# An expert's outputs in the other order: the 64-row half made and added first, the 128-row half second

## The chip, the cores and the metric

The kernel runs on one core of one Trainium2 chip. The metric is the time of one launch on the device in microseconds (us); of several runs the median counts, and less is better. A core has five engines that follow their own instruction streams and meet at semaphores only: PE (TensorE, matrix products; its weight loads are listed as PEld), DVE (VectorE), ACT (ScalarE), POOL (GpSimd) and SP (SyncE). Sixteen DMA engines move data between the chip's memory (DRAM) and the on-chip memory; SP issues the plain loads (queue q1 of the profile), POOL the indirect ones (queue q0).

## The reference

One decoder layer over 32 sequences of 128 tokens, width 512: a normed differential attention with rotary embedding, a cross attention to a context of 128 rows per sequence, and a mixture of experts. Cut to the part that the change touches, the mixture of experts does this for its T = 4096 tokens and E = 48 kept experts:

```
logits = x @ gate_weight.T                    # experts that are not kept: -inf
top_v, top_i = top_k(softmax(logits), 8); top_v /= sum(top_v)
xb[e, 0:192] = the first 192 tokens that chose expert e      # capacity 192
g, u = split(xb @ gate_up_proj.T);  h = silu(g) * u          # 192 wide
y = h @ down_proj.T                                          # 512 wide
out[token] += weight * y                                     # over the chosen experts
```

All numbers are FP32. A token can be among several experts' rows, so two experts' additions can meet in one row of the output.

## The kernel before

It has two stages. The first (up to about 690 us) takes the 32 sequences through attention, cross attention and routing, one sequence per turn, several sequences in flight. It writes the residual rows to the output in DRAM and scatters each token's record (normed row, weights, token number) to the slots of its experts. The second stage takes the 48 experts, and the change lies there alone.

An expert has 192 slots, cut into a half of 128 rows (h = 0) and a half of 64 rows (h = 1). Each engine runs `expert_turn` once per turn; in one turn the engines work on three experts at once: `t` (rows are transposed and split), `u` (gate and up product, L1382, and the activation) and `d` (down product, L1416). FP32 products are made from a high and a low part, which is why every operand is copied (ACT, L693) and its rest subtracted (DVE, L1133).

The way of an expert's outputs:

- PE (L1405 to L1418) makes both halves one after the other, five products each, in two banks of its result memory: half 0 in bank 4 (128 rows), half 1 in bank 5 (64 rows). It counts each half on the semaphore `down_tensor`; the object `dwn_t` (L355) names the order of the counts. Before it overwrites a bank it waits until that half of the expert before was copied out.
- ACT (L821 to L825) copies half 0 to the buffer `y` (called qk_both in the profile) and scales it with the slots' weights; DVE (L1172 to L1177) does the same for half 1. `y` has room for two experts, so both wait until the additions of the expert before the last are through (`d_add`, L824 and L1175).
- POOL (L680 to L687) adds the rows to the output in DRAM with one indirect DMA for each half (`add_outputs`, L670 to L678): each row goes to the row of its token, and the DMA adds. Since two experts can meet in a row, POOL waits at L683 until both additions of the expert before have landed. The order is: that wait, the wait for half 0, its addition, the wait for half 1, its addition.

SP loads each expert's data ahead: `load_gate_up` (L436, 768 KB), `load_down` (L442, 256 KB), `load_rows` (L454 and L456, 280.5 and 140.2 KB). Each waits until its buffer is free, which DVE signals (L1141, L1181, L1193). The order on every engine is as written in the code; nothing is moved by a scheduler.

Of the kernel before, what the change touches and what calls it, by code (L numbers as in the profile page):

```python
# [86 lines left out]
def decoder_layer(nc, x, ctx_rows, ctx_t, mask, weights, lambdas, subln, gate, gate_up, down_proj,  # L87
# [9 lines left out]
    with stack:  # L97
# [254 lines left out]
        ffn_a = Steps(sem("rows_scalar"), "high0 high1")  # L352
        ffn_v = Steps(sem("rows_vector"), "low0 low1")
        ffn_w = Steps(sem("rows_vector_kept"), "tokens weight")
        dwn_t = Steps(sem("down_tensor"), "y0 y1")  # L355
        dwn_v = Steps(sem("down_vector"), "y1")
        dwn_a = Steps(sem("down_scalar"), "y0")

# [195 lines left out]
        def _(pool):  # L554
# [125 lines left out]
            for e in range(E):  # L680
                d = Batch(e // 2, e % 2, E)
                if d.back(1).exists():
                    pool.wait_ge(d_add[d.back(1).parity], moved(d.back(1), 2))  # L683
                pool.wait_ge(dwn_a.sem, dwn_a.after(d, "y0"))
                add_outputs(d, 0)
                pool.wait_ge(dwn_v.sem, dwn_v.after(d, "y1"))
                add_outputs(d, 1)  # L687

        @block.scalar
        def _(act):  # L690
# [101 lines left out]
            def expert_turn(b):  # L792
                t, u, d = b["turn"], b["up"], b["down"]
                if t.exists():
                    act.wait_ge(d_gu[t.parity], moved(t, 1))
                    if t.back(2).exists():
                        act.wait_ge(gup_t.sem, gup_t.after(t.back(2), "second"))
                    copy(gu_high[:, t.parity, :, :], gu_sb[:, t.parity, :, :], wgu_a)
                if u.exists():
                    act.wait_ge(gup_t.sem, gup_t.after(u, "first"))  # L800
                    if u.back(1).exists():
                        act.wait_ge(gup_v.sem, gup_v.after(u.back(1), "h2"))
                    act.activation(silu1[:, :], ps[:, 2, 0:CAP], ACT.Silu).then_inc(gup_a.sem, 1)
                    act.wait_ge(gup_t.sem, gup_t.after(u, "second"))
                    act.activation(silu2[:, :], ps[0:INTER - P, 3, 0:CAP], ACT.Silu).then_inc(gup_a.sem, 1)
                if t.exists():
                    for h in range(2):
                        act.wait_ge(ffn_t.sem, ffn_t.after(t, f"rowsT{h}"))
                        if t.back(2).exists():
                            act.wait_ge(gup_t.sem, gup_t.after(t.back(2), "second"))  # L810
                        copy(rows_high[:, t.parity, :, part(h)],
                             ps[:, h, 0:KC * PART[h]].rearrange("p (c n) -> p c n", c=KC), ffn_a)
                if u.exists():
                    if u.back(2).exists():
                        act.wait_ge(dwn_t.sem, dwn_t.after(u.back(2), "y1"))
                    for h, dst, name in ((h1, h1_high, "h1"), (h2, h2_high, "h2")):
                        act.wait_ge(gup_v.sem, gup_v.after(u, name))
                        copy(dst[:, u.parity, 0, :], h[:, :], gup_a)
                    copy(h2_again[:, u.parity, 0, :], h2[:, :], gup_a)
                if d.exists():  # L820
                    act.wait_ge(dwn_t.sem, dwn_t.after(d, "y0"))  # L821
                    act.wait_ge(ffn_w.sem, ffn_w.after(d, "weight"))
                    if d.back(2).exists():
                        act.wait_ge(d_add[d.back(2).parity], moved(d.back(2), 2))  # L824
                    copy(y[:, d.parity, 0, :], ps[:, 4, :], dwn_a, scale=weight_of[d.parity][:, 0:1])  # L825
                if u.exists():
                    act.wait_ge(d_dn[u.parity], moved(u, 1))
                    if u.first():
                        act.wait_ge(d_dn2, 16 * 3)
                    if u.back(2).exists():  # L830
                        act.wait_ge(dwn_t.sem, dwn_t.after(u.back(2), "y1"))
                    copy(dn_high[:, u.parity, 0, :], dn_sb[:, u.parity, :], wdn_a)
                    copy(dn2_high(u), dn2_raw(u), wdn_a)
            expert_turns(act, expert_turn)
# [2 lines left out]
        def _(dve):  # L837
# [297 lines left out]
            def expert_turn(b):  # L1135
# [24 lines left out]
                                rows_high[:, t.parity, :, part(h)]).then_inc(ffn_v.sem, 1)  # L1160
                if u.exists():
                    if u.back(2).exists():
                        dve.wait_ge(dwn_t.sem, dwn_t.after(u.back(2), "y1"))
                    dve.wait_ge(gup_a.sem, gup_a.after(u, "high1"))
                    left_by(h1_low[:, u.parity, 0, :], h1[:, :], h1_high[:, u.parity, 0, :]).then_inc(gup_v.sem, 1)
                    dve.wait_ge(gup_a.sem, gup_a.after(u, "high2"))
                    if u.first():
                        for parity in range(2):
                            dve.memset(h2_rest[HALVES[1 - parity], parity, 0, :].bitcast(FP32), 0.0)
                    left_by(h2_low(u), h2[:, :], h2_high[:, u.parity, 0, :]).then_inc(gup_v.sem, 1)  # L1170
# [28 lines left out]
        def _(pe):  # L1199
# [165 lines left out]
            def expert_turn(b):  # L1365
                t, u, d = b["turn"], b["up"], b["down"]
                if u.exists():
                    if u.first():
                        keep_busy(2, 6)
                    if u.is_(1):  # L1370
                        keep_busy(3, 6)
                    pe.wait_ge(wgu_v.sem, wgu_v.after(u, "low"))
                    pe.wait_ge(ffn_v.sem, ffn_v.after(u, "low1"))
                    if u.back(1).exists():
                        pe.wait_ge(gup_v.sem, gup_v.after(u.back(1), "h2"))

                    def gate_up_block(dst, m):
                        cols = slice(m * P, (m + 1) * P)
                        pairs = [(gu_high, rows_high), (gu_high, rows_low), (gu_low, rows_high)]
                        for n, (left, right) in enumerate(pairs):  # L1380
                            for k in range(KC):
                                last = pe.matmul(dst, left[:, u.parity, k, cols], right[:, u.parity, k, :],  # L1382
                                                 start=(n == 0 and k == 0), stop=(n == 2 and k == KC - 1))
                        return last
                    for m in range(2):
                        last = gate_up_block(ps[:, 2, m * CAP:(m + 1) * CAP], m)
                    last.then_inc(gup_t.sem, 1)
                    gate_up_block(ps[:, 3, 0:CAP], 2).then_inc(gup_t.sem, 1)
                if t.exists():
                    if t.first():  # L1390
                        keep_busy(18)
                    pe.wait_ge(d_rows[t.parity], moved(t, 2))
                    if t.back(1).exists():
                        pe.wait_ge(ffn_v.sem, ffn_v.after(t.back(1), "low1"))
                    for h in range(2):
                        for c in range(KC):
                            n = PART[h]
                            last = pe.transpose(ps[:, h, c * n:(c + 1) * n], rows[0:n, t.parity, h, c * P:(c + 1) * P],
                                                ident[0:n, 0:n])
                        last.then_inc(ffn_t.sem, 1)  # L1400
                if d.exists():
                    pe.wait_ge(wdn_v.sem, wdn_v.after(d, "low2"))
                    pe.wait_ge(gup_v.sem, gup_v.after(d, "low2"))
                    pe.wait_ge(gup_a.sem, gup_a.after(d, "again"))
                    for h in range(2):  # L1405
                        if h == 0:
                            if d.back(1).exists():
                                pe.wait_ge(dwn_a.sem, dwn_a.after(d.back(1), "y0"))
                        else:
                            if d.back(1).exists():  # L1410
                                pe.wait_ge(dwn_v.sem, dwn_v.after(d.back(1), "y1"))
                        dst = ps[0:PART[h], 4 + h, :]
                        pairs = [(h1_high, dn_high, P), (h1_high, dn_low, P), (h1_low, dn_high, P),
                                 (h2_twice, dn2_both, P), (h2_rest, dn2_both, P)]
                        for i, (left, right, n) in enumerate(pairs):
                            last = pe.matmul(dst, left[0:n, d.parity, 0, part(h)], right[0:n, d.parity, 0, :],  # L1416
                                             start=(i == 0), stop=(i == len(pairs) - 1))
                        last.then_inc(dwn_t.sem, 1)  # L1418
# [55 lines left out]
```

## Time and profile before

| | us |
|---|---|
| median of 3 runs | 1086.99 (1086.17 to 1087.95) |
| the profiled execution | 1082.65 |
| its span, first to last instruction | 1080.9 |
| first addition of outputs starts | 704.27 |
| last addition of outputs starts | 1075.11 |

Over the whole span PE is busy for 94%, DVE for 77%, ACT for 58%, POOL for 54%. These shares are means over two stages with different limits, so they do not tell what limits the expert stage. The page also follows the work that ended last backwards to what released it; there 52% of the span is PE's and 22% is the additions to the output (layer_out), in flight as DMAs. An addition appears in the profile twice: as POOL's instruction at L672, which lasts while POOL writes the DMA's orders, and as the DMA itself, whose time is told from the start of that instruction to its landing.

### The profile page before, as it was taken

What the parts mean: (1) busy time and instruction counts of PE and PEld (TensorE: products, weight loads), DVE (VectorE), ACT (ScalarE), POOL (GpSimd) and SP (SyncE); (2) the same over time, 40 slices, a digit from 0 to 9 for tenths busy, and PEclk for the clock granted to TensorE, in tenths of its full rate; (3) what the DMA queues carried; (4) which work ended last, traced back from release to release, by engine and by line L of the source; (5) the groups of instructions that cost most, each with busy time, mean ns of one, the idle gap of its engine ahead of it and who ended that gap; (6) DMA issues with size and microseconds to landing.
All of it is one profiled execution on the core that took longest, in us unless ns stands there. A gap on an engine that the chain in (4) does not pass through costs nothing.

```text
span 1080.9 us, 24325 instructions
## 1 busy us (share of the span) xinstructions
PE 1020.4 (94%) x6564; PEld 830.6 (77%) x6564; DVE 832.9 (77%) x2255; ACT 625.6 (58%) x1751; POOL 579.1 (54%) x565
## 2 busy tenths in 40 slices
PE   5999999999999999999999987999999999999993
PEld 3787778878878788778787875788888787877882
DVE  5678778878888788788887865588888878778782
ACT  4555455455455554554555541477767676676772
POOL 3224665676666666766666666434444343443444
PEclk9999999999999999999999999999999999999997
DMA  7999674543313112122134132489999999989984
GB/s 285 370 294 265 248 262 158 212 153 129 131 56 99 49 54 92 49 81 65 49 97 166 55 122 79 135 234 257 239 248 234 239 235 230 247 217 238 240 203 58
DMA packets 90644, 185.75 MB, mean 172 GB/s; under 512 B 23943, under 2 KB 24071, under 8 KB 89712
## 3 DMA queue, kind: packets, MB, share of 16 engines
q1 hardware_dynamic: 59232, 145.13, 41.2%
q0 software_dynamic: 31376, 40.20, 18.0%
q8 instruction: 16, 0.26, 0.1%
q14 instruction: 20, 0.16, 0.0%
HBM read 116.04 MB, written 122.00 MB: 220 GB/s over the span
## 4 chain that ended last, share of the span: by engine, by line
PE 52%; DMA 27%; issue 10%; POOL 5%; DVE 3%; ACT 1%; SPq 0%; POOLq 0%; DVEq 0%
PE ps L1226 27%; DMA layer_out<-qk_both,slot_table 22%; PE ps L1211 9%; PE ps L1216 4%; DMA arena<-in_x 4%; PE ps L1253 3%; PE ps L1324 2%; POOL layer_out L672 2%; PE ps L1357 2%; POOL slot_records L587 2%; PE ps L1382 2%; PE ps L1416 1%; DMA gu_sb<-in_weights 1%; POOL rstd L598 1%; DMA arena<-slot_records 1%
## 5 line engine op out<-in xcount | busy, mean ns | idle before, releaser
L587 POOL DMA_INDIRECT slot_records<-row,slot_idx x240 | 245.2, 1022 | 78.5 <-issue 50.0
L672 POOL DMA_INDIRECT layer_out<-qk_both,slot_table x96 | 161.6, 1683 | 223.2 <-DMA layer_out<-qk_both,slot_table 196.0
L598 POOL TENSOR_TENSOR rstd<-mv,neg_half 128x1 f32<-128x1 f32 x96 | 67.8, 707 | 121.4 <-DVE mv L966 78.5
L1226 PE MATMUL ps<-w_high,xn_high 128*128 128x512 f32 x384 | 114.1, 419 | 0.7 <-ACT xn_high L693 0.7
L728 ACT ACTIVATE arena<-ps,neg_max 128x128 f32<-128x128 f32 x256 | 90.1, 378 | 33.4 <-DVE neg_max L958 33.4
L1226 PE MATMUL ps<-w_low,xn_high 128*128 128x512 f32 x384 | 107.7, 403 | 0.0
L1226 PE MATMUL ps<-w_high,xn_low 128*128 128x512 f32 x384 | 106.7, 399 | 0.0
L1382 PE MATMUL ps<-w_high 128*128 128x192 f32 x576 | 89.7, 278 | 13.4 <-DVE w_low L1133 13.0
L1382 PEld LDWEIGHTS ps<-w_high 128*128 128x128 f32 x576 | 76.7, 191 | 30.2 <-issue 28.3
L1133 DVE TENSOR_TENSOR w_low<-gu_sb,w_high 128x1536 fp32r<-128x1536 f32 x48 | 84.4, 1758 | 16.1 <-ACT w_high L693 14.9
L693 ACT ACTIVATE xn_t<-ps 128x512 f32<-128x512 f32 x64 | 38.3, 599 | 98.9 <-PE ps L1211 98.8
L1382 PE MATMUL ps<-w_high,w_low 128*128 128x192 f32 x576 | 87.8, 274 | 0.0
L1382 PE MATMUL ps<-w_low,w_high 128*128 128x192 f32 x576 | 87.7, 274 | 0.0
L1416 PE MATMUL ps<-w_high 128*128 128x512 f32 x192 | 80.4, 419 | 2.6 <-DVE w_high L1133 2.6
L1226 PEld LDWEIGHTS ps<-w_low,xn_high 128*128 128x128 f32 x384 | 70.9, 191 | 14.1
L1226 PEld LDWEIGHTS ps<-w_high,xn_low 128*128 128x128 f32 x384 | 70.1, 189 | 13.6
L643 POOL TENSOR_TENSOR arena<-qk_both 128x256 f32<-128x256 f32 x64 | 46.5, 745 | 60.0 <-DVE qk_both L1048 60.0
L1211 PEld LDWEIGHTS ps<-ident,arena 128*128 128x128 f32 x392 | 43.3, 142 | 43.5 <-ACT arena L693 17.0
L1048 DVE TENSOR_TENSOR qk_both<-ps,rope_tab 128x1024 f32<-128x1024 f32 x64 | 75.2, 1217 | 1.2 <-PE ps L1226 1.2
L1382 PEld LDWEIGHTS ps<-w_low,w_high 128*128 128x128 f32 x576 | 75.9, 192 | 0.0
L1382 PEld LDWEIGHTS ps<-w_high,w_low 128*128 128x128 f32 x576 | 75.9, 192 | 0.0
L1211 PE MATMUL ps<-ident,arena 128*128 128x128 f32 x392 | 61.9, 284 | 14.1 <-ACT arena L740 8.9
(164 smaller groups left out, 2477.0 us busy)
## 6 DMA issues: line engine op xcount, KB each, us to landing
gu_sb<-in_gate_up SPq DMA_DIRECT2D x48, 768.0 KB, 5.9
slot_records<-arena SPq DMA_DIRECT2D x6, 3366.0 KB, 25.0
arena<-slot_records SPq DMA_DIRECT2D x48, 280.5 KB, 4.4
dn_sb<-in_down_proj SPq DMA_DIRECT2D x48, 256.0 KB, 3.7
arena<-in_x SPq DMA_DIRECT2D x32, 256.0 KB, 2.7
x_res<-in_x SPq DMA_DIRECT2D x32, 256.0 KB, 3.0
ctx_t_sb<-in_ctx_t SPq DMA_DIRECT2D x32, 256.0 KB
ctx_sb<-in_ctx_rows SPq DMA_DIRECT2D x32, 256.0 KB
```

The source lines that it names most:

```text
L587: pool.indirect_dma_start(out=records, out_offset=bass.IndirectOffsetOnAxis(ap=slot_idx_of(s)[:, k:k + 1], axis=0), in_=row_of(s), in_offs ...
L598: pool.tensor_tensor(rstd[:, :], mv[:, 1:2], neg_half[:, 0:1], ALU.pow).then_inc(steps.sem, 1)
L643: pool.tensor_tensor(qk_rot[:, g, 1, :], qk_cos[:, g, 1, :], qk_sin[:, g, 0, :], ALU.add).then_inc(rope_p.sem, 1)
L672: pool.indirect_dma_start(out=out, out_offset=bass.IndirectOffsetOnAxis(ap=slot_table[0:PART[h], 2 * d.index + h:2 * d.index + h + 1], axi ...
L728: last = act.activation(probs[:, s, h, :], blocks(banks_s[:, s, :])[:, h, :], ACT.Exp, bias=neg_max[:, s, h:h + 1], accum_out=prob_sum[:, ...
L1048: dve.tensor_tensor(buf[:, :, :, :].rearrange("p (a g) r f -> p a (g r) f", a=2), qk, rope_tab[:, i, :, :].unsqueeze(2).to_broadcast([P, 2 ...
L1133: return dve.tensor_tensor(dst, src, high.bitcast(FP32), ALU.subtract)
L1211: last = pe.transpose(blocks(bank)[:, c, :], src(c), ident[:, :])
L1216: last = pe.matmul(dst, left(c), right(c), start=(c == 0), stop=(c == n - 1))
L1226: last = pe.matmul(dst, left[:, c, :], right[:, m, c, :], start=(n == 0 and c == 0), stop=(n == 2 and c == KC - 1))
L1382: last = pe.matmul(dst, left[:, u.parity, k, cols], right[:, u.parity, k, :], start=(n == 0 and k == 0), stop=(n == 2 and k == KC - 1))
L1416: last = pe.matmul(dst, left[0:n, d.parity, 0, part(h)], right[0:n, d.parity, 0, :], start=(i == 0), stop=(i == len(pairs) - 1))
```

## The change

The two halves of an expert's outputs change places, in what PE makes first and in what POOL adds first. The counts of `down_tensor` are renamed to match, so that ACT still waits for half 0 and DVE for half 1, and so that "both halves are made" is still the second count (now called y0). ACT's and DVE's own order is as before.

```diff
-        dwn_t = Steps(sem("down_tensor"), "y0 y1")
+        dwn_t = Steps(sem("down_tensor"), "y1 y0")
...
                 if d.back(1).exists():
                     pool.wait_ge(d_add[d.back(1).parity], moved(d.back(1), 2))
+                pool.wait_ge(dwn_v.sem, dwn_v.after(d, "y1"))
+                add_outputs(d, 1)
                 pool.wait_ge(dwn_a.sem, dwn_a.after(d, "y0"))
                 add_outputs(d, 0)
-                pool.wait_ge(dwn_v.sem, dwn_v.after(d, "y1"))
-                add_outputs(d, 1)
...
                     if u.back(2).exists():
-                        act.wait_ge(dwn_t.sem, dwn_t.after(u.back(2), "y1"))
+                        act.wait_ge(dwn_t.sem, dwn_t.after(u.back(2), "y0"))
...
                     if u.back(2).exists():
-                        dve.wait_ge(dwn_t.sem, dwn_t.after(u.back(2), "y1"))
+                        dve.wait_ge(dwn_t.sem, dwn_t.after(u.back(2), "y0"))
...
-                    for h in range(2):
+                    for h in (1, 0):
                         if h == 0:
                             if d.back(1).exists():
                                 pe.wait_ge(dwn_a.sem, dwn_a.after(d.back(1), "y0"))
```

On POOL, at the start of the second stage, the additions of the first three experts stood in this order before. A row is one addition; down_scalar is the signal that half 0 (128 rows) was copied out, down_vector that of half 1 (64 rows), and outputs_added the landing of the expert before.

```order
L672 DMA layer_out<-qk_both,slot_table 4352x512 [waits residual_stored1,residual_stored0,down_scalar]
L672 DMA layer_out<-qk_both,slot_table 4352x512 [waits down_vector]
L672 DMA layer_out<-qk_both,slot_table 4352x512 [waits down_scalar,outputs_added0]
L672 DMA layer_out<-qk_both,slot_table 4352x512 [waits down_vector]
L672 DMA layer_out<-qk_both,slot_table 4352x512 [waits down_scalar,outputs_added1]
```

The same place in the changed kernel:

```order
L672 DMA layer_out<-qk_both,slot_table 4352x512 [waits residual_stored1,residual_stored0,down_vector]
L672 DMA layer_out<-qk_both,slot_table 4352x512 [waits down_scalar]
L672 DMA layer_out<-qk_both,slot_table 4352x512 [waits down_vector,outputs_added0]
L672 DMA layer_out<-qk_both,slot_table 4352x512 [waits down_scalar]
L672 DMA layer_out<-qk_both,slot_table 4352x512 [waits down_vector,outputs_added1]
```

The wait for the landing of the expert before now stands in front of the 64-row addition, and the 128-row addition is the last of each expert.

On PE, in an expert's turn, the down product stood before as follows, between the transposes of a later expert's rows (L1398) and the next turn's first gate product (L1382). The number of rows is the first of the two sizes.

```order
L1398 MATMUL ps<-ident,arena 128x64 x4
L1416 MATMUL ps<-w_high 128x512
L1416 MATMUL ps<-w_low,w_high 128x512
L1416 MATMUL ps<-w_high,w_low 128x512
L1416 MATMUL ps<-w_high 128x512
L1416 MATMUL ps<-w_high,w_low 128x512
L1416 MATMUL ps<-w_high 64x512
L1416 MATMUL ps<-w_low,w_high 64x512
L1416 MATMUL ps<-w_high,w_low 64x512
L1416 MATMUL ps<-w_high 64x512
L1416 MATMUL ps<-w_high,w_low 64x512
L1382 MATMUL ps<-w_high 128x192 x4
```

In the changed kernel:

```order
L1398 MATMUL ps<-ident,arena 128x64 x4
L1416 MATMUL ps<-w_high 64x512
L1416 MATMUL ps<-w_low,w_high 64x512
L1416 MATMUL ps<-w_high,w_low 64x512
L1416 MATMUL ps<-w_high 64x512
L1416 MATMUL ps<-w_high,w_low 64x512
L1416 MATMUL ps<-w_high 128x512
L1416 MATMUL ps<-w_low,w_high 128x512
L1416 MATMUL ps<-w_high,w_low 128x512
L1416 MATMUL ps<-w_high 128x512
L1416 MATMUL ps<-w_high,w_low 128x512
L1382 MATMUL ps<-w_high 128x192 x4
```

The five products of the 64-row half moved ahead of the five of the 128-row half; the instructions are the same.

## Rows read from the trace of the kernel before

**Rows 1.** Busy time by stretch of the expert stage (columns named in the first row)

```profile
core 0: us, PE busy (x) PEld busy (x) DVE busy (x) ACT busy (x) POOL busy (x), PEclk, DMA share, GB/s
704.00:742.00 38.00, 38.00 (x283) 33.31 (x282) 31.77 (x62) 29.44 (x58) 15.89 (x9) 1.00 0.90 236
742.00:1048.00 306.00, 292.82 (x2108) 247.09 (x2107) 246.19 (x468) 217.35 (x427) 130.38 (x78) 1.00 0.93 237
1048.00:1081.00 33.00, 15.53 (x102) 12.21 (x100) 12.32 (x25) 11.25 (x23) 15.33 (x10) 0.82 0.49 68
```

**Rows 2.** Instructions of L672 over the span, what POOL waited for (us, times)

```profile
L672 POOL DMA_INDIRECT layer_out<-qk_both,slot_table x96: 1424/1567/2188, 704.3 to 1075.1; - x96
...
  DMA layer_out<-qk_both,slot_table: 196.0, 47
```

**Rows 3.** Chain that ended last (start us, us, what it was)

```profile
738.52 2.51 PE ps L1416 x10
...
850.70 5.84 DMA layer_out<-qk_both,slot_table
...
1062.60 4.18 DMA layer_out<-qk_both,slot_table
```

**Rows 4.** Timeline of POOL (start us, us, instruction, idle time before and what ended it)

```profile
704.27 1.57 POOL L672 DMA_INDIRECT layer_out<-qk_both,slot_table  x1 [12.57 <-ACT qk_both L695]
...
848.83 1.56 POOL L672 DMA_INDIRECT layer_out<-qk_both,slot_table  x1 [4.24 <-DMA layer_out<-qk_both,slot_table]
850.70 1.72 POOL L672 DMA_INDIRECT layer_out<-qk_both,slot_table  x1 [0.30 <-issue]
856.80 1.57 POOL L672 DMA_INDIRECT layer_out<-qk_both,slot_table  x1 [4.38 <-DMA layer_out<-qk_both,slot_table]
...
1047.92 1.56 POOL L672 DMA_INDIRECT layer_out<-qk_both,slot_table  x1 [3.84 <-DMA layer_out<-qk_both,slot_table]
...
1060.74 1.56 POOL L672 DMA_INDIRECT layer_out<-qk_both,slot_table  x1 [3.07 <-DMA layer_out<-qk_both,slot_table]
1062.60 1.43 POOL L672 DMA_INDIRECT layer_out<-qk_both,slot_table  x1 [0.30 <-issue]
1067.04 1.56 POOL L672 DMA_INDIRECT layer_out<-qk_both,slot_table  x1 [3.02 <-DMA layer_out<-qk_both,slot_table]
```

**Rows 5.** Instructions of L672, 848.5 to 849.5 us: one 128-row addition's landing

```profile
DMA to landing us min/median/max: 4.8/4.8/4.8
```

**Rows 6.** Instructions of L672, 1060 to 1061 us: the same near the end

```profile
DMA to landing us min/median/max: 4.9/4.9/4.9
```

**Rows 7.** DMA queues, 851 to 852.5 us (packets, MB, share of 16 engines)

```profile
q0 software_dynamic: 87, 0.18, 95.6%
q1 hardware_dynamic: 1, 0.00, 0.0%
```

**Rows 8.** DMA queues, 854 to 855.25 us

```profile
q1 hardware_dynamic: 110, 0.23, 54.0%
q0 software_dynamic: 63, 0.11, 47.4%
```

**Rows 9.** Timeline, all engines: loads and copies around one expert, and the first expert

```profile
703.09 0.73 DVE L1133 TENSOR_TENSOR w_low<-h,w_high 128x192 fp32r<-128x192 f32 x2
703.30 0.69 ACT L695 ACTIVATE qk_both<-ps,weight_even 128x512 f32<-128x512 f32 x1
...
850.57 0.33 SPq L442 DMA_DIRECT2D dn_sb<-in_down_proj  x1
...
853.53 0.34 SPq L436 DMA_DIRECT2D gu_sb<-in_gate_up  x1
...
856.56 0.69 ACT L695 ACTIVATE qk_both<-ps,weight_even 128x512 f32<-128x512 f32 x1 [1.77 <-DMA layer_out<-qk_both,slot_table]
856.56 0.74 DVE L1176 TENSOR_SCALAR qk_both<-ps,weight_even 64x512 f32<-64x512 f32 x1 [0.86 <-DMA layer_out<-qk_both,slot_table]
```

**Rows 10.** The page's slices of the span, 27 us each: memory traffic

```profile
GB/s 285 370 294 265 248 262 158 212 153 129 131 56 99 49 54 92 49 81 65 49 97 166 55 122 79 135 234 257 239 248 234 239 235 230 247 217 238 240 203 58
```

More of the change, by code:

```diff
@@ L830, in expert_turn @@
                     if u.back(2).exists():
-                        act.wait_ge(dwn_t.sem, dwn_t.after(u.back(2), "y1"))
+                        act.wait_ge(dwn_t.sem, dwn_t.after(u.back(2), "y0"))
                     copy(dn_high[:, u.parity, 0, :], dn_sb[:, u.parity, :], wdn_a)
```

## The prediction

> **What bounds the kernel now.** I first read the chain of work that ended last. After PE's last down product there, at 738.52 us, it names nothing but additions to the output in flight, each followed by a short step on POOL; the reader sees one such addition per expert [rows 3]. The instructions of L672 say the same from POOL's side: of its 48 experts, 47 began after a wait for a landing of the expert before, 196.0 us in all [rows 2]. So the 48 pairs of additions form one chain from 704.27 us to the end. Third, the timeline of POOL gives one link of it: the first addition starts at 848.83 us, issues for 1.56 us, the second starts 0.31 us later at 850.70, lands 5.84 us after its start, at 856.54, and 0.26 us later POOL starts the next expert at 856.80 [rows 3, 4]. That is 0.26 + 1.56 + 0.31 + 5.84 = 7.97 us. Over the first 43 experts the mean is (1047.92 - 704.27) / 43 = 7.99 us; near the end, with no loads left, it is 1067.04 - 1060.74 = 6.30 us [rows 4].
>
> What matters in that sum is which landing ends it. The 128-row addition, issued first, lands 4.8 us after its start [rows 5], at 853.6; POOL does not wait for that, since the 64-row one lands 2.9 us later.
>
> The copies to `y` are ready in time: at 856.56 ACT and DVE copy out an expert after waiting 1.77 and 0.86 us for the very landing that also frees POOL [rows 9]. PE is close behind with 292.82 of 306 us busy between 742 and 1048 us, the DMA engines with a share of 0.93 [rows 1]. Neither gives the beat now, but both are near enough to be rivals.
>
> **The change part by part.** It removes no instruction and no byte. It decides which addition is issued last.
>
> *The first issue gets shorter, the second longer.* Without loads the 64-row issue takes 1.43 us and the 128-row one 1.56 us [rows 4]: -0.13 us at the first place, +0.13 us within the landing time of the second. In the loaded stretch the second issue took 1.72 us for 64 rows [rows 4], 0.29 more than near the end; I take this as bound to the place, so whichever half stands there pays it. If it grows with the rows, 0.29 us more per expert.
>
> *The last landing is now that of 128 rows.* Near the end I have both sizes nearly undisturbed: 4.9 us for 128 rows [rows 6], 4.18 for 64 [rows 3]. An expert's link there becomes -0.13 + (4.9 - 4.18) = +0.59 us longer. For the 43 loaded experts no row shows a 128-row addition in the second place, so I bound it. From below: the extra 64 rows cost no more than undisturbed, +0.59 us. From above: the loaded 64-row landing is 5.84 - 4.18 = 1.66 us longer than the undisturbed one, of which the issue is 0.29 and the crowd 1.37; if twice the rows meet twice the crowd, +0.59 + 1.37 = +1.96 us. A gain is excluded as long as rows take DMA time at all; the rival below says what if they don't.
>
> Between these ends the row on the queues decides. While the first addition's rows move, they have the engines nearly alone: q0 95.6%, the loads' q1 0.0% [rows 7]. While the second one's rows move, q0 has 47.4% and q1 54.0% [rows 8], since the load issued at 850.57 has begun and the 768 KB load issued at 853.53 is about to [rows 9]. So the small half moves into the free stretch, where nobody waits for it, and the large half into the shared one. At that share the extra rows need 0.59 / 0.47 = 1.26 us. The share does not hold for the whole of a longer transfer, as the loads pause between two issues, so I take the middle of 0.59 and 1.26, 0.93 us.
>
> The Trainium skill, "DMA: Bandwidth & Descriptors", "Queues, rings and completion order", says that a DMA engine takes turns between queues and drains a whole packet, typically 9 to 17 descriptors, before it switches. An expert's rows on one engine would then pass in one go, and the crowd would be met once: the lower end, +0.59 us, and 1116 us in all. The trace shows only that both queues hold about half over 1.25 us [rows 8], not in what grain.
>
> *PE's order.* PE makes the 64 rows first. ACT's copy of half 0 becomes possible later by the five products of the other half; in the loaded stretch ACT waits 1.77 us for the landing anyway [rows 9], which covers it, and the copy runs a whole expert ahead of POOL. Uncovered it would hold up ACT's weight copies behind it by about 1.25 us, half of the 2.51 us that the ten products of both halves take [rows 3]. The renamed waits still ask for the second count, so DVE's and ACT's splits of a later expert wait as before. SP's waits are untouched.
>
> *The first addition.* Before, it waited for ACT's copy at 703.30 [rows 4, 9]. Now it needs DVE's copy, and DVE is busy with two subtractions from 703.09 for 0.73 us [rows 9], then copies for 0.74: POOL starts at about 704.8 instead of 704.27, +0.5 us once.
>
> *Sum.* 0.5 + 43 x 0.93 + 5 x 0.59 = 0.5 + 40.0 + 3.0 = 43.5 us. Against the profiled execution's own 1082.65 us (1080.9 of span and 1.75 around it) that is 1126.1; the median of the runs is 4.3 us above that execution, so 1086.99 + 43.5 = 1130 us.
>
> **The rivals.**
> 1. *Only the bytes count.* The extra 128 KB move at the fastest rate that a slice shows, 370 GB/s [rows 10], in 0.35 us; per expert +0.35, in all 0.5 + 48 x 0.35 = 17 us, 1104 us. For: the slices of the expert stage lie below that rate. Against: the undisturbed landings differ by 0.72 us, of which only 0.13 is issue. The Trainium skill, same page, "Anatomy of one DMA — SWDGE (gpsimd) path", has a fit of this kind, 2.0 us plus the bytes over 436 GB/s; as an estimate it puts the extra rows at 0.30 us, and 0.5 + 48 x 0.30 = 15 us in all. The trace speaks against it by the same 0.72 us.
> 2. *Faster: the crowd sets the last landing, not the rows.* Of the 5.84 us, 1.66 are there only in company. If the second addition ends when the loads let its last row through, however many rows it has, then only the shorter first issue is left: 0.5 - 48 x 0.13 = -5.7 us, 1081 us. It decides from the point where 64 more rows lengthen the landing by under 0.13 us. For: the loads' queue holds over half there [rows 8]. Against: near the end, with no loads, the rows do cost 0.59 us.
> 3. *No change: the DMA engines set the beat.* A share of 0.93 of 7.99 us is 7.4 us of transfers per expert; were that the limit, their order would not matter, 1087 us. For: the share [rows 1]. Against: POOL waits 47 times for a landing, also near the end, where the share is 0.49 [rows 1, 2].
> 4. *Much slower.* Twice the rows meet twice the crowd, +1.96 us: 0.5 + 43 x 1.96 + 3 = 88 us, 1175 us. PE would then idle some 2 us per expert; its granted clock is 1.00 through the stage and 0.82 only over the last 33 us, of which it is busy for 15.5 [rows 1], so a fall of the clock to its lower level, 1.2 GHz, would belong to this case.
>
> **How the numbers follow.** The forecast, from +0.59 to about +1.6 us per expert (1116 to 1160 us), gets 0.74; rival 1 0.08, rival 2 0.07, rival 3 0.06, rival 4 0.05. What this measurement can tell from no change is about 0.2%, 2 us. Faster is rival 2, 0.07; same is rival 3, 0.06; slower is the rest, 0.87. The range from 1104 to 1160 us holds the forecast and most of rival 1, about 8 in 10.
>
> **What would show it.** In the changed profile the first issue should take 1.43 us; near the end a link of 6.9 us instead of 6.30, its last landing 4.9 us after the start of the 128-row addition; in the loaded stretch a link of about 8.9 us, with the last landing about 6.9 us after that start; the DMA share between 742 us and the end of the loads near 0.83 (7.43 us of transfers in 8.92), PE idle for more than a tenth of it at a granted clock of 1.00. The prediction is wrong if the loaded link stays at 8.0 us, if POOL waits for a copy instead of a landing, or if loads move in time so that the 128 rows find the engines free.

## The result, and the profile after

The changed kernel takes 1113.82 us (median of 6 runs, 1108.84 to 1115.08) against 1086.93 for the kernel before: a ratio of 1.0239, 95% interval 1.0218 to 1.0260, so 24 to 28 us slower. The forecast was 1130 us, range 1104 to 1160.

The profiled span grew by more than the medians, from 1080.9 to 1112.8 us. Of these 31.9 us, 3.41 lie before the first addition, which starts at 707.68 us and not at 704.27. Most of that is not the change's: PE's first down product already starts 2.81 us later there, and in profiles of kernels that make and add the 128-row half first, this first addition starts anywhere between 704 and 710 us.

The expert stage by stretch (columns as in [rows 1]):

```profile
707.00:745.00 38.00, 37.96 (x283) 32.97 (x282) 31.35 (x61) 28.63 (x56) 13.50 (x8) 1.00 0.90 234
745.00:1077.00 332.00, 294.25 (x2111) 246.82 (x2110) 248.78 (x469) 214.66 (x430) 120.10 (x78) 1.00 0.88 220
1077.00:1113.00 36.00, 16.38 (x99) 12.66 (x97) 12.71 (x25) 11.30 (x23) 15.54 (x10) 0.78 0.45 62
```

Nearly the same work takes 332 us in place of 306. PE is idle for 11% of it where it was idle for 4, at a granted clock of 1.00 (2.4 GHz), and the DMA engines' share fell from 0.93 to 0.88. No engine became clearly busier; the waits grew. The instructions of L672 after (answers to [rows 2]):

```profile
L672 POOL DMA_INDIRECT layer_out<-qk_both,slot_table x96: 1419/1550/2790, 707.7 to 1106.6; - x96
...
  DMA layer_out<-qk_both,slot_table: 236.7, 47
...
  DVE qk_both L1176: 13.2, 1
```

All 47 waits are still for a landing, now 236.7 us instead of 196.0, and POOL's first wait is for DVE's copy instead of ACT's. The timeline of POOL after, one link and the two ends of the first 43 experts (answers to [rows 4]):

```profile
707.68 1.48 POOL L672 DMA_INDIRECT layer_out<-qk_both,slot_table  x1 [13.17 <-DVE qk_both L1176]
...
933.67 1.42 POOL L672 DMA_INDIRECT layer_out<-qk_both,slot_table  x1 [5.01 <-DMA layer_out<-qk_both,slot_table]
935.40 1.56 POOL L672 DMA_INDIRECT layer_out<-qk_both,slot_table  x1 [0.30 <-issue]
941.99 1.42 POOL L672 DMA_INDIRECT layer_out<-qk_both,slot_table  x1 [5.04 <-DMA layer_out<-qk_both,slot_table]
...
1077.10 1.43 POOL L672 DMA_INDIRECT layer_out<-qk_both,slot_table  x1 [4.81 <-DMA layer_out<-qk_both,slot_table]
```

The chain that ended last, in a loaded link and near the end (answers to [rows 3]):

```profile
935.40 6.33 DMA layer_out<-qk_both,slot_table
...
1093.28 4.56 DMA layer_out<-qk_both,slot_table
```

And the landing of the 64-row addition that starts at 933.67, from the instructions of L672 between 933.6 and 934 us (answers to [rows 5]):

```profile
DMA to landing us min/median/max: 3.6/3.6/3.6
```

The 64 rows land at 937.3, with nobody waiting; the 128 rows land at 941.73, and POOL goes on 0.26 us later. The loaded link has a mean of (1077.10 - 707.68) / 43 = 8.59 us where it had 7.99 [rows 4]. So the account of the chain is 43 x 0.60 = 25.8 us, 5 x 0.55 = 2.7 for the last five, and some 0.6 us at the first addition, 29.1 in one pair of executions against the 26.9 of the medians.

Split into its steps, as means over the experts 6 to 42, worked out from the starts and lengths of the instructions at L672 and their landings in the traces:

| us | link | first issue | second issue | end of second issue to landing |
|---|---|---|---|---|
| before | 7.92 | 1.56 | 1.82 | 3.93 |
| after | 8.52 | 1.42 | 1.65 | 4.84 |
| difference | +0.60 | -0.14 | -0.17 | +0.91 |

The rest of a link, the two short steps between, is about 0.61 us in both. The 128 rows do cost 0.91 us more in the shared stretch. The queues between 938 and 940.5 us, while they move, show that stretch shared here too, with the larger part the additions' (q0); [rows 8] is half as long a window and had 47.4 and 54.0%:

```profile
q0 software_dynamic: 114, 0.22, 57.8%
q1 hardware_dynamic: 127, 0.27, 36.6%
```

What I had not forecast is the second issue: a 128-row issue in that place is shorter than the 64-row one was. The timeline of DVE before, ahead of the second issue that starts at 850.70 [rows 4], and after, at the one that starts at 935.40, has the reason in view. Before:

```profile
850.43 0.69 DVE L1133 TENSOR_TENSOR w_high<-arena,w_high 64x512 fp32r<-64x512 f32 x1
```

After:

```profile
935.39 0.73 DVE L1133 TENSOR_TENSOR w_high<-arena,w_high 64x512 fp32r<-64x512 f32 x1
```

Before, DVE's last weight subtraction of an expert starts 0.27 us ahead of POOL's issue, and the issue takes 1.72 us. After, the first issue is 0.14 us shorter, POOL starts its second within 0.01 us of the subtraction, and the issue takes its undisturbed 1.56. In the changed kernel's own timeline there is an expert that shows the other outcome, POOL and DVE around 825.8 us:

```profile
825.72 0.69 DVE L1133 TENSOR_TENSOR w_high<-arena,w_high 64x512 fp32r<-64x512 f32 x1
825.81 2.03 POOL L672 DMA_INDIRECT layer_out<-qk_both,slot_table  x1 [0.30 <-issue]
```

Here DVE came 0.09 us first and the issue took 2.03 us. Eight of the 37 experts 6 to 42 lost in this way after; before, 36 of 37 did.

### The profile page after: what moved, and what is told of

Its sections match the earlier page's. It is cut to its first block, busy times and chain, and to the rows that moved or that the text cites. A ratio compares the mean times of both kernels' runs of the same rounds, so it can differ in the third digit from the quotient of the medians.

```text
span 1112.8 us, 24325 instructions
## 1 busy us (share of the span) xinstructions
PE 1026.1 (92%) x6564; PEld 834.0 (75%) x6564; DVE 834.8 (75%) x2255; ACT 621.6 (56%) x1751; POOL 565.6 (51%) x565
## 4 chain that ended last, share of the span: by engine, by line
PE 51%; DMA 32%; issue 9%; POOL 5%; DVE 2%; ACT 1%; POOLq 0%; SPq 0%; DVEq 0%
PE ps L1226 28%; DMA layer_out<-qk_both,slot_table 27%; PE ps L1211 9%; PE ps L1216 5%; DMA arena<-in_x 3%; PE ps L1253 3%; POOL layer_out L672 3%; PE ps L1324 2%; PE ps L1357 2%; POOL slot_records L587 1%; DMA gu_sb<-in_weights 1%; PE ps L1382 1%; POOL rstd L598 0%; PE ps L1233 0%; PE ps L1341 0%
## 5 line engine op out<-in xcount | busy, mean ns | idle before, releaser
L672 POOL DMA_INDIRECT layer_out<-qk_both,slot_table x96 | 149.1, 1554 | 264.5 <-DMA layer_out<-qk_both,slot_table 236.7
L1382 PE MATMUL ps<-w_high 128*128 128x192 f32 x576 | 90.9, 280 | 37.0 <-DVE w_low L1133 36.2
L1382 PEld LDWEIGHTS ps<-w_high 128*128 128x128 f32 x576 | 75.9, 191 | 55.4 <-issue 55.0
L1382 PE MATMUL ps<-w_high,w_low 128*128 128x192 f32 x576 | 87.8, 274 | 0.0
L1382 PE MATMUL ps<-w_low,w_high 128*128 128x192 f32 x576 | 87.6, 274 | 0.0
L1416 PE MATMUL ps<-w_high 128*64 128x512 f32 x192 | 78.3, 408 | 5.8 <-DVE w_high L1133 5.3
L1382 PEld LDWEIGHTS ps<-w_low,w_high 128*128 128x128 f32 x576 | 75.9, 192 | 0.0
L1382 PEld LDWEIGHTS ps<-w_high,w_low 128*128 128x128 f32 x576 | 75.9, 192 | 0.0
L1416 PE MATMUL ps<-w_high,w_low 128*64 128x512 f32 x192 | 75.7, 394 | 0.0
```

The lines of the kernel that those rows point to most:

```text
L672: pool.indirect_dma_start(out=out, out_offset=bass.IndirectOffsetOnAxis(ap=slot_table[0:PART[h], 2 * d.index + h:2 * d.index + h + 1], axi ...
```

## The experiments

For the loss, three theories had to be told apart: *order of landing* (only POOL's order counts, through the rows of the last addition and the loads beside them), PE's order, and DMA engines that set the beat. For the length of the second issue there were two: *port* (POOL's issue waits for DVE's subtraction if that runs already), and rows of the first addition in flight that slow the second issue.

**POOL's order alone.** The kernel before with only the lines of POOL from the change.

```diff
+                pool.wait_ge(dwn_v.sem, dwn_v.after(d, "y1"))
+                add_outputs(d, 1)
                 pool.wait_ge(dwn_a.sem, dwn_a.after(d, "y0"))
                 add_outputs(d, 0)
-                pool.wait_ge(dwn_v.sem, dwn_v.after(d, "y1"))
-                add_outputs(d, 1)
```

> Only POOL's order is changed (64-row addition first); PE still makes the 128-row half first. If all of the loss lies in which addition lands last, this loses as much as the whole change: 1110 to 1116 us, a link of the chain of about 8.6 us between 750 and 1045 us. If PE's order (half 0 ready later, ACT's copies behind it) carries part of the loss, it stays below 1105 us. If the DMA engines set the beat, 1087 us.

Measured 1113.27 us, ratio 1.0236 (1.0189 to 1.0282), link 8.53 us: the whole loss, as the first theory had it.

**PE's order alone.** The changed kernel with POOL's lines put back.

```diff
-                pool.wait_ge(dwn_v.sem, dwn_v.after(d, "y1"))
-                add_outputs(d, 1)
                 pool.wait_ge(dwn_a.sem, dwn_a.after(d, "y0"))
                 add_outputs(d, 0)
+                pool.wait_ge(dwn_v.sem, dwn_v.after(d, "y1"))
+                add_outputs(d, 1)
```

> Only PE's order is changed; POOL still adds the 128-row half first. If the loss lies in which addition lands last, this is as before: 1085 to 1089 us, link 8.0 us. If PE's order costs something by itself, over 1090 us.

Measured 1087.26 us, ratio 1.0016 (0.9993 to 1.0040), link 7.91 us: no difference that can be told. PE's part of the change is free.

**A useless instruction on DVE.** The kernel before, with a fill ahead of the subtraction.

```diff
+                    dve.memset(squares[:, 0:2, :], 0.0)
                     dve.wait_ge(wdn_a.sem, wdn_a.after(u, "high2"))
                     left_by(dn2_low(u), dn2_raw(u), dn2_high(u)).then_inc(wdn_v.sem, 1)
```

> The kernel before, with one useless VectorE fill (128x256, about 0.3 us) put ahead of the last weight subtraction (64x512) of each expert. Port theory: POOL's second issue takes 1.7 to 1.9 us instead of 1.43 because this subtraction is already running when the issue starts; started later it no longer holds the issue up, which falls to about 1.43 us, the link from 8.0 to about 7.6 us, the time to 1068 to 1075 us, although work was added. Rival: the issue is long because the 128 rows of the first addition are moving meanwhile; then it stays at 1.7 to 1.9 us and the time at 1087 us or above.

Measured 1077.14 us, ratio 0.9916 (0.9884 to 0.9948): faster than both kernels, by 0.5 to 1.2% against the kernel before, with one instruction more per expert, though 2 us above the expected range. The timeline of POOL and DVE in it, at two experts one after the other:

```profile
783.79 0.69 DVE L1133 TENSOR_TENSOR w_high<-arena,w_high 64x512 fp32r<-64x512 f32 x1
783.89 1.91 POOL L672 DMA_INDIRECT layer_out<-qk_both,slot_table  x1 [0.30 <-issue]
...
791.17 0.27 DVE L1182 MEMSET squares<- 128x256 f32 x1
791.34 1.43 POOL L672 DMA_INDIRECT layer_out<-qk_both,slot_table  x1 [0.30 <-issue]
791.46 0.69 DVE L1133 TENSOR_TENSOR w_high<-arena,w_high 64x512 fp32r<-64x512 f32 x1
```

At the first of them the subtraction is still 0.10 us ahead of the issue, which takes 1.91 us (3 of 37 experts); at the second it comes 0.12 us behind, and the issue takes 1.43. The 128 rows of the first addition are in flight both times. So for the length of the issue the port theory stands and its rival falls. The mean issue fell by 0.35 us (1.82 to 1.47), the link by 0.27 (7.92 to 7.65); 0.08 came back between the issue and the landing. That the link's gain is all the issue's is not shown by this run: the fill also moves the row loads behind it, from 3.21 to 3.43 us after the landing of the expert before, and the last experiment shows that these count too. For the issue speaks the changed kernel itself: its 8 experts with a long second issue have links of 9.06 us in the mean, the other 29 of 8.37, while the row loads start at nearly the same time (3.21 and 3.26 us, medians); but eight experts are few.

**The same fill in the changed kernel.** With the race taken out of both kernels, the pair shows the price of the order alone.

```diff
+                    dve.memset(squares[:, 0:2, :], 0.0)
                     dve.wait_ge(wdn_a.sem, wdn_a.after(u, "high2"))
```

> The changed kernel with the same useless VectorE fill as x3_before_pad. Without it the change was measured with a gift: its second issue starts 0.13 us earlier and so mostly escapes VectorE's subtraction, which the kernel before meets nearly always. With the fill in both, neither meets it, and the pair shows the price of the order alone. Port theory: against x3_before_pad (1077 us) this kernel takes 1110 to 1115 us, 33 to 38 us more, a link of 8.45 instead of 7.65 us. Rival (the gift is something else, the order costs 27 us in any company): 1102 to 1105 us.

Measured 1111.21 us, ratio 1.0212 (1.0163 to 1.0262) to the kernel before, which makes 1.0212 / 0.9916 = 1.030 to the kernel before with the fill, some 32 us; the 33 to 38 expected lie within the noise of the two intervals. Link 8.41 against 7.65 us: +0.76, of which the landing after the issue is 0.82 (4.83 against 4.01). The second issues, all 1.56 us now, are +0.09 and the first -0.14. Without the race the change costs a quarter more per link than it did (0.76 against 0.60).

**Smaller loads.** In both kernels, from the third expert on, three quarters of the gate and up weights are not loaded, so these kernels leave out part of the work; they serve for times alone.

```diff
-                sp.dma_start(gu_sb[:, e.parity, :, :], gate_up[bass.ds(e.index * P, P), :, :])\
+                chunks = slice(0, KC) if e.is_(0) or e.is_(1) else slice(0, 1)
+                sp.dma_start(gu_sb[:, e.parity, chunks, :], gate_up[bass.ds(e.index * P, P), chunks, :])\
```

> The kernel before; from the third expert on only a quarter of the gate and up weights is loaded (192 of 768 KB), the rest stays what the buffer held, so the outputs of those experts are not the reference's. Crowd theory: the second addition (64 rows) lands about 4.2 to 4.6 us after its start instead of 5.75, the chain falls under PE's beat of 7.33 us per expert, and the time to 1055 to 1065 us. If the landing does not depend on the loads: 5.75 us, 1087 us.

> The changed kernel with the same quarter of the gate and up weights. Crowd theory: the last addition (128 rows) lands about 4.9 to 5.3 us after its start instead of 6.5, the link is 7.0 to 7.4 us, near PE's beat, and the time within 8 us of x6_before_quarter: the order costs little where the loads are small. Rival (128 rows cost what they cost in any company): 6.5 us to the landing, link 8.5 us, 1105 us or more.

Measured 1063.79 and 1070.13 us (two runs each). In the kernel before with the small loads, 742 to 1030 us (columns as in [rows 1]):

```profile
742.00:1030.00 288.00, 288.00 (x2126) 251.43 (x2125) 243.56 (x472) 219.77 (x434) 148.68 (x79) 1.00 0.80 176
```

In the changed kernel with the small loads:

```profile
742.00:1030.00 288.00, 288.00 (x2105) 247.56 (x2105) 246.29 (x469) 218.59 (x430) 136.01 (x78) 1.00 0.83 174
```

PE is busy without a break in both, with links of 7.36 and 7.38 us: PE sets the beat, and the order makes no difference to it. POOL still waits for a landing ahead of every expert; what gives way is its first issue, with a mean of 2.38 us in the kernel before and 1.89 in the changed one, instead of 1.56 and 1.42. For most experts it starts while DVE's 128x1536 subtraction of gate and up weights runs, and is held as the second issue was by the smaller subtraction. In the kernel before with the small loads (line numbers are one higher there):

```profile
880.50 1.75 DVE L1134 TENSOR_TENSOR w_low<-gu_sb,w_high 128x1536 fp32r<-128x1536 f32 x1
881.47 2.21 POOL L673 DMA_INDIRECT layer_out<-qk_both,slot_table  x1 [3.25 <-DMA layer_out<-qk_both,slot_table]
```

The issue ends 1.43 us after the subtraction, and in all 33 of the experts 6 to 42 where that subtraction ran first it is 1.43 to 1.45 us. In the changed kernel the landing is longer and this hold shorter, and the beat stays. Second addition of one expert, from its start, in the kernel before with the small loads:

```profile
DMA to landing us min/median/max: 4.2/4.2/4.2
```

And in the changed kernel with the small loads:

```profile
DMA to landing us min/median/max: 4.9/4.9/4.9
```

These are the nearly undisturbed times of [rows 3] and [rows 6]; the means over the experts 6 to 42 are 4.38 and 4.88 us. From the end of the issue the means are 2.94 and 3.31 us: the 64 rows more cost 0.37 us there and 0.91 us in the company of the full loads. The 6 us between the two kernels arise outside this stretch: their profiles put the first addition 1.5 us apart, the first five links together 1.8 us, and the last five links are 6.60 and 6.97 us long.

**Halves of 96 rows.** The kernel before with both halves of one size.

```diff
-        PART = (P, CAP - P)
+        PART = (HS, HS)
...
-            return slice(h * P, h * P + PART[h])
+            return slice(h * HS, (h + 1) * HS)
```

(and the same size in the row loads and in ACT's copy)

> The kernel before with two equal halves of 96 rows instead of 128 and 64. Rows theory: the landing after the end of the second issue lies between that of 64 rows (3.9 us) and that of 128 (4.85), near 4.4 us; the second issue still meets VectorE's subtraction (1.8 to 1.95 us), so the link is about 8.4 us and the time 1100 to 1108 us. If it is the order of PE or of the waits and not the rows of the last addition, 1087 us. If only a last addition of full 128 rows hurts, under 1092 us.

Measured 1093.31 us, ratio 1.0043 (1.0018 to 1.0069), link 8.11 us: between the two, as the rows theory has it, but 7 us under the expected range. The time alone would hardly tell it from the third case expected (under 1092 us); the landing does. The landing after the issue is 4.58 us (64 rows 3.93, 128 rows 4.84). What I missed is the race again: the first issue of 96 rows takes 1.41 us, so the second starts early enough for 28 of the 37 experts, and its mean is 1.52 us, not 1.8 to 1.95.

**Can the race be won for nothing?** The two small copies of DVE moved ahead of the subtraction, instead of a fill.

```diff
+                if t.exists():
+                    dve.wait_ge(d_rows[t.parity], moved(t, 2))
+                    dve.tensor_copy(slot_table[:, bass.ds(2 * t.index, 2)],
...
+                    dve.tensor_copy(weight_of[t.parity][:, :],
...
-                    dve.wait_ge(wdn_a.sem, wdn_a.after(u, "high2"))
-                    left_by(dn2_low(u), dn2_raw(u), dn2_high(u)).then_inc(wdn_v.sem, 1)
+                if u.exists():
+                    dve.wait_ge(wdn_a.sem, wdn_a.after(u, "high2"))
+                    left_by(dn2_low(u), dn2_raw(u), dn2_high(u)).then_inc(wdn_v.sem, 1)
```

> The kernel before, with VectorE's two small copies of slots and weights put ahead of the last weight subtraction instead of behind it; no work added. Port theory: the subtraction starts about 0.25 us later, behind the start of POOL's second issue, which falls to about 1.43 us; time 1066 to 1075 us. The row loads are then issued about 0.6 us earlier, which could take back up to 0.3 us per expert (1085 us). Rival (rows of the first addition in flight lengthen the issue): 1.7 to 1.9 us stays, 1087 us.

Measured 1090.24 us, ratio 1.0038 (1.0013 to 1.0063): no gain, where 1066 to 1075 us were expected and 1085 at most. The second issue did fall, to a mean of 1.55 us (10 of the 37 experts still met the subtraction), but the landing then took 4.26 us instead of 3.93, and the link is 7.97. What differs from the fill is that the copies also free SP's row loads (L454), which then start earlier. Two more kernels take that apart: fill and moved copies together, and, on the kernel before, a fill of twice the length, whose edit is shown.

```diff
+                    dve.memset(squares[:, 0:4, :], 0.0)
                     dve.wait_ge(wdn_a.sem, wdn_a.after(u, "high2"))
```

> The kernel before with both the fill of x3_before_pad and the moved copies of x4_before_moved. The second issue escapes VectorE's subtraction for every expert (1.43 us), as the subtraction starts about 0.4 us after it. It differs from x3_before_pad in one more thing: the row loads are issued about 3.06 us after the landing of the expert before, as in x4_before_moved, not 3.42 us. If the earlier row loads are what took back the gain in x4_before_moved, the landing takes about 4.25 us from the end of the issue, the link 7.85 us, the time 1083 to 1088 us. If not, 4.0 us, 7.6 us and 1072 to 1077 us.

> The kernel before with a fill twice as long (128x512, about 0.55 us) at the same place as in x3_before_pad. All second issues take 1.43 us, the row loads come about 3.7 us after the landing of the expert before, the 768 KB load about 0.1 to 0.3 us later than in x3_before_pad. If later row loads leave the last addition more room: link 7.45 to 7.6 us, 1068 to 1075 us. If the added work now delays the loads that PE waits for: link 7.7 us or more, 1078 us or more.

Measured 1090.66 us, ratio 1.0015 (0.9998 to 1.0031), and 1078.93 us, ratio 0.9920 (0.9895 to 0.9944): the first shows no difference from the kernel before, the second none from the short fill, and both lie above the ranges expected for a gain. In order of the start of the row loads (from the landing of the expert before to SP's instruction at L454; all columns are means over the experts 6 to 42):

| us | row loads start | second issue | end of issue to landing | link |
|---|---|---|---|---|
| fill and moved copies | 2.92 | 1.43 | 4.34 | 7.94 |
| moved copies | 2.93 | 1.55 | 4.26 | 7.97 |
| kernel before | 3.21 | 1.82 | 3.93 | 7.92 |
| fill | 3.43 | 1.47 | 4.01 | 7.65 |
| longer fill | 3.77 | 1.45 | 4.03 | 7.66 |

The timeline of POOL and SP in the kernel with fill and moved copies:

```profile
948.38 1.56 POOL L672 DMA_INDIRECT layer_out<-qk_both,slot_table  x1 [4.18 <-DMA layer_out<-qk_both,slot_table]
950.24 1.43 POOL L672 DMA_INDIRECT layer_out<-qk_both,slot_table  x1 [0.30 <-issue]
950.92 0.33 SPq L454 DMA_DIRECT2D arena<-slot_records  x1
```

And in the kernel with the fill alone:

```profile
950.53 1.43 POOL L672 DMA_INDIRECT layer_out<-qk_both,slot_table  x1 [0.30 <-issue]
951.83 0.34 SPq L454 DMA_DIRECT2D arena<-slot_records  x1
```

The row loads start 0.68 us after the second addition's issue began in the one and 1.30 us after in the other. The queues from 2.5 to 3.5 us after the start of that issue show what follows. With fill and moved copies (952.74 to 953.74 us):

```profile
q1 hardware_dynamic: 135, 0.26, 87.7%
q0 software_dynamic: 9, 0.02, 10.0%
```

With the fill alone (953.03 to 954.03 us):

```profile
q0 software_dynamic: 43, 0.08, 57.6%
q1 hardware_dynamic: 85, 0.15, 46.6%
```

So in the first of the two most of that stretch is the loads', and in the second over half is the addition's. Over the experts 6 to 42 the additions move 20 KB in it in the one kernel and 67 KB in the other, as means worked out from the packets in the traces; 64 rows have 128 KB. Where the row loads come early, all of the shorter issue is lost again before the landing; where they come later, the link is shorter, and later still gives nothing more. The row loads are the only loads that start earlier in the one than in the other (the 256 KB load starts 2.13 us after the landing of the expert before in both), so it is they that take this room from the last addition. What is not shown is how much of the fill's 0.27 us per link is the shorter issue's and how much the later row loads': no run has the kernel before's row loads with the short issue.

The fastest kernel that does all of the work is the one with the short fill, 1077.14 us; the longer fill's 1078.93 cannot be told from it.

## Why the prediction was right, and where its size was off

- *What bounds the kernel:* right. The chain of additions is the bound in both kernels, and POOL's order alone carries the loss.
- *First issue -0.13 us:* measured -0.14.
- *The extra rows near the end, +0.59 us per link:* measured +0.55 (6.86 against 6.31 us, mean of the last five); the landing of the last three experts comes 4.56 to 4.81 us after the start, where 4.9 was foretold.
- *The extra rows in the shared stretch:* my 0.93 us per link was this term alone, with the two issues cancelling. From the end of the second issue to the landing it measured 0.91 us. The small loads show that company makes a good part of it: 0.37 us with a quarter of the gate and up weights, and 0.59 near the end of the stage. The size is right by luck in part: it was the middle of two bounds, and nothing in the working picks the middle.
- *The second issue, +0.13 us:* this is the term that was mis-sized. I bound the long issue to its place, whichever half stands there. It is bound to a race with DVE that the shorter first issue wins for 29 of 37 experts, and it measured -0.17 us. The 0.30 us between the two, 43 times, is 13 of the 16.6 us by which the forecast was too high (43.5 us forecast, 26.9 measured); 2.2 more lie between the pair of profiled executions and the medians.
- *PE's order at nothing:* right, 1.0016 (0.9993 to 1.0040). *The first addition +0.5 us:* about 0.6 once PE's later start there is taken off.
- *DMA share and PE:* 0.88, not 0.83, since the link is 8.52 and not 8.92 us; PE idle for 11% at a clock of 1.00, as foretold.
- *Rival 1, bytes alone:* +0.35 us per link would leave the landing after the issue at 4.3 us; it is 4.84. *Rival 2, faster:* its 1081 us fell with the landing. *Rival 3, DMA engines set the beat:* fell with POOL's order alone. *Rival 4, +1.96 us:* did not occur.

The total is near the 1116 us that I had put beside the Trainium skill's rule on packets ("DMA: Bandwidth & Descriptors", "Queues, rings and completion order"). That agreement is an accident of the race: the rule as I read it would have the crowd met once, and the rows measured 0.91 us and not 0.59.

## What to carry to other kernels

When two transfers of different size are issued one behind the other and waited for together, look which one lands last. Here it was the one issued last, and putting the larger one first, where its transfer runs beside the issue of the other, was worth 0.60 us per pair, 0.76 without the race. Before costing a moved issue by its place, look which engine's instruction was running when it started; 0.1 us decided a race that is worth 0.3 to 0.5 us of issue. And a shorter step on the chain is kept only if nothing else, here a load released by the same edit, moves into the room.

## What the runs showed of the hardware

POOL's indirect issue does not go on while DVE's subtraction of two operands in on-chip memory runs, if the subtraction was first: started 0.27 us into the subtraction the 64-row issue takes 1.72 us instead of 1.43, and the 128-row issue 0.09 us into it 2.03 instead of 1.56. When both start within 0.02 us of each other, or POOL is first, it takes its 1.43 or 1.56 us. With the small loads the 128-row issue ended 1.43 to 1.45 us after the end of DVE's subtraction, 33 times of 33. A fill that is running on DVE does not hold it up. The timeline of DVE and POOL in the kernel with the longer fill, where the fill runs 0.36 us into the issue:

```profile
952.12 0.48 DVE L1182 MEMSET squares<- 128x512 f32 x1
952.24 1.43 POOL L672 DMA_INDIRECT layer_out<-qk_both,slot_table  x1 [0.30 <-issue]
```

The Trainium skill, "SBUF — State Buffer", "SBUF: two separate sides", says that DVE and POOL share a pair of ports under an exclusive lock, that whoever starts first keeps it for the whole instruction, and that a DVE instruction with two inputs in that memory conflicts only with a POOL one that reads it. The trace agrees on who waits when DVE is first. When POOL is first, DVE does not wait out POOL's instruction: 0.12 us behind it the subtraction takes its usual 0.69 us, and 0.73 when both start together, so here nothing is held for POOL's whole instruction.
